# Moving the value splits and the clearing of the block-diagonal values of a rotary attention into the last turn of the cross-attention before it

## What is computed

```python
x = x + _L1_xattn_ref(_layernorm(x, axis=-1), ctx_1024, L1_xattn_Wq, ...)
x = x + _L1_attn_ref(_layernorm(x, axis=-1), L1_attn_Wq, ..., L1_attn_Wo, L1_attn_bo)
# _L1_attn_ref, 16 heads of 64:
q = _apply_rope((x @ Wq + bq).reshape(b, s, H, L), cos, sin)
k = _apply_rope((x @ Wk + bk).reshape(b, s, H, L), cos, sin)
v = (x @ Wv + bv).reshape(b, s, H, L)
attn = softmax(where(causal, q @ k.T / sqrt(L), -1e9))
return (attn @ v).reshape(b, s, H * L) @ Wo + bo
```

## Time and profile before

| | us |
|---|---|
| median of three executions | 1123.29 |
| lowest, highest | 1121.62, 1125.1 |
| the profiled execution, its own time | 1119.95 |
| its span, first to last instruction | 1118.2 |
| matmul busy in the span | 1062.4 (95%) |
| VectorE, ScalarE, GpSimd busy | 639.4, 346.6, 214.2 |

### The profile page before, as it was taken

One profiled execution on the slowest core, in us unless ns is written; L12 is line 12 of the kernel. 1 busy time (PEld: TensorE's weight loads), 2 busy tenths in 40 slices (PEclk: granted clock), 3 DMA queues, 4 the chain that ended last, 5 costly groups with the idle time before them and its releaser, 6 DMA issues.

```text
span 1118.2 us, 16788 instructions
## 1 busy us (share of the span) xinstructions
PE 1062.4 (95%) x6152; PEld 662.9 (59%) x6152; DVE 639.4 (57%) x1105; ACT 346.6 (31%) x982; POOL 214.2 (19%) x205
## 2 busy tenths in 40 slices
PE   7999999999899999999999999999789999999777
PEld 4466658888444444444444565559479796878233
DVE  2454346787756621456751354476756758477667
ACT  1232246666420000220000132244412525135443
POOL 0111101333122221000004311124204132130004
PEclk9999999999999999999999999999899999999899
DMA  9966902001025690025537579941000000040001
GB/s 335 386 250 220 367 3 76 1 1 39 19 93 184 128 38 1 0 91 181 151 103 273 185 264 372 349 169 51 1 1 1 1 0 0 1 166 1 1 1 75
DMA packets 67585, 128.01 MB, mean 114 GB/s; under 512 B 9296, under 2 KB 13136, under 8 KB 67152
## 3 DMA queue, kind: packets, MB, share of 16 engines
q1 hardware_dynamic: 67536, 127.38, 35.4%
HBM read 120.92 MB, written 6.44 MB: 114 GB/s over the span
## 4 chain that ended last, share of the span: by engine, by line
PE 69%; issue 11%; DVE 8%; POOL 5%; SPq 2%; DMA 2%; ACT 1%; POOLq 0%; DVEq 0%; ACTq 0%
PE bank L2075 24%; PE bank L449 5%; PE bank L2102 5%; PE bank L937 4%; PE bank L419 4%; PE bank L380 3%; PE bank L2284 3%; PE bank L944 2%; PE bank L1623 2%; PE bank L1554 2%; PE bank L494 2%; PE bank L483 2%; DMA xres<-in_x_dram 1%; PE bank L953 1%; PE bank L1563 1%
## 5 line engine op out<-in xcount | busy, mean ns | idle before, releaser
L2120 ACT ACTIVATE f_act<-bank,f_sgn 128x512 f32<-128x512 f32 x64 | 44.0, 687 | 266.1 <-PE bank L2075 253.8
L2075 PE MATMUL bank<-f_a_lo,f_w 128*128 128x512 f16 x512 | 115.7, 379 | 0.0
L2075 PE MATMUL bank<-f_a_hi,f_w 128*128 128x512 f16 x512 | 115.7, 379 | 0.0
L2075 PEld LDWEIGHTS bank<-f_a_lo,f_w 128*128 x512 | 50.1, 98 | 60.4
L2075 PEld LDWEIGHTS bank<-f_a_hi,f_w 128*128 x512 | 50.1, 98 | 60.2
L2174 DVE CAST f_b_hi<-f_act 128x512 f16<-128x512 f32 x32 | 26.1, 817 | 96.3 <-ACT f_act L2120 96.3
L1833 DVE TENSOR_TENSOR s_e<-s_pair,s_tables 128x512 f32<-128x512 f32 x64 | 41.4, 689 | 44.2 <-POOL s_qT L1912 15.2
L419 PE MATMUL bank<-x_cT,x_qT 128*64 128x512 f32 x256 | 60.1, 613 | 0.0
L449 PE MATMUL bank<-x_cN,x_eT 128*64 128x512 f32 x256 | 56.9, 596 | 0.0
L1712 ACT ACTIVATE s_e<-bank,s_nmax 128x64 f32<-128x64 f32 x128 | 38.1, 337 | 33.4 <-DVE s_nmax L1775 33.2
L2223 POOL TENSOR_SCALAR f_w<-f_upper_bits 128x2048 bf16<-128x2048 uint8 x16 | 30.8, 1928 | 81.8 <-PE bank L2075 81.8
(11 more groups left out here) (331 smaller groups left out, 2304.9 us busy)
## 6 DMA issues: line engine op xcount, KB each, us to landing
x_cT<-in_ctx_cols_dram SPq DMA_DIRECT2D x32, 1024.0 KB, 9.0
x_cN<-in_ctx_rows_dram SPq DMA_DIRECT2D x32, 1024.0 KB, 10.9
f_upper_bits<-in_f_w_dram SPq DMA_DIRECT2D x20, 256.0 KB, 3.9
f_row<-in_f_wg_dram SPq DMA_DIRECT2D x11, 256.0 KB, 3.5
f_long_row<-in_f_wd_dram SPq DMA_DIRECT2D x4, 704.0 KB, 5.9
f_row<-in_f_wu_dram SPq DMA_DIRECT2D x11, 256.0 KB, 2.8
f_part<-in_f_wgT_dram SPq DMA_DIRECT2D x8, 352.0 KB, 3.5
f_part<-in_f_wuT_dram SPq DMA_DIRECT2D x8, 352.0 KB, 3.4
```

The costliest lines, as they stand in the source:

```text
L2075: mm = pe.matmul(h_bank[s][:, :], weights(2 * i + s, k), part[:, k, cols], start=(n == 0 and k == 0), stop=(n == 1 and k == k_chunks - 1))
L2120: act.activation(act32[s][:, :], h_bank[s][:, :], ACT.Relu, scale=sgn[:, layer % 2:layer % 2 + 1]).then_inc(h_read, 1)
```

## The change

- The clearing of `v_diag` moves from the start of the rotary attention (GpSimd) into the cross-attention's last turn, behind the two bias additions L779 and ahead of the two additions L1351. Its semaphore moves with it.
- High part 2 goes ahead of the copy L551 of the second tile's transposed weights, parts 3 and 4 ahead of the two scaled outputs; only part 5 is left behind the casts L572.
- Low parts 1 to 4 are made ahead of L710, and part 5 ahead of both last additions to x.
- Low part 6 moves from VectorE ahead of step 3 to GpSimd behind its eight rotary steps, ahead of `rstd`.
- The high value weights and the raw and low output weights swap places, so the output weights now lie on the second tile's context rows and their load waits for `av_done, TILES`.

```diff
@@ sync, cross-attention
                 successor.load_values(sp)
-                sp.wait_ge(av_done, TILES - 1)
+                sp.wait_ge(av_done, TILES)
                 successor.load_outputs(sp)
@@ scalar, cross-attention, loop over s with the exponentials
+                    if s == 1 and last and successor is not None:
+                        act.wait_ge(s_done, TILES)
+                        successor.split_hi(act, 2)
                     if proj is None:
                         act.wait_ge(eT_done, 2 * i + s + 1)
                         act.copy(eT[s][:, :, :], as_chunks(bank[ET_BANK[s]][:, :])).then_inc(eT_ok, 1)
@@
                 for s in range(2):
                     if last and successor is not None:
-                        act.wait_ge(s_done, TILES)
-                        successor.split_hi(act, 2 + s)
+                        successor.split_hi(act, 3 + s)
                     act.wait_ge(av_done, 2 * i + s + 1)
@@
                 if last and successor is not None:
-                    successor.split_hi(act, 4)
                     successor.split_hi(act, 5)
@@ vector, cross-attention
                 if last and successor is not None:
-                    for n in range(1, 4):
+                    for n in range(1, 5):
                         successor.split_lo(dve, n)
@@
                 for s in range(2):
-                    if s and last and successor is not None:
-                        successor.split_lo(dve, 4)
+                    if s == 0 and last and successor is not None:
+                        successor.split_lo(dve, 5)
                     dve.wait_ge(y_done, 2 * i + s + 1)
@@ gpsimd, cross-attention
                 pool.wait_ge(successor.small_in, 16 * successor.N_SMALL)
+                pool.wait_ge(xn_ok, TILES + 1)
+                pool.wait_ge(xb_ok, TILES)
+                successor.clear_values(pool)
                 for s in range(2):
                     pool.wait_ge(xn_ok, TILES + s + 1)
                     successor.add_bias(pool, xres, s)
@@ RotaryFront
+    def clear_values(self, pool):
+        pool.memset(self.v_diag[:, :, :, :, :], 0.0).then_inc(self.set_ok, 1)
@@ vector, rotary attention
-            dve.wait_ge(set_ok, 1)
+            dve.wait_ge(rot.set_ok, 1)
@@
                 for n in range(2 * GROUPS):
-                    if first and n in (1, 3):
-
-                        rot.split_lo(dve, 5 + n // 2)
                     if n in (4, 5):
@@ gpsimd, rotary attention
-            pool.wait_ge(*x_done)
-            pool.memset(v_diag[:, :, :, :, :], 0.0).then_inc(set_ok, 1)
-
@@
+                if first:
+                    rot.split_lo(pool, 3 * NB)
                 if last:
                     ffn.roots(pool, 0, 0, TILES - 2)
```

More of the change, by code:

```diff
@@ L1251, in __init__ @@
             self.wv_raw = first("wv_raw", [P, KC, F])
+            first("over_v_hi", [P, KC, F])
             self.wo_raw = first("wo_raw", [P, FC, D])
-            for n in ("over_v_hi", "over_k_hi"):
-                first(n, [P, KC, F])
+            first("over_k_hi", [P, KC, F])
             Front.reserve(first, "raw_over_front")
@@ L1260, in __init__ @@
             self.wk_lo, self.wq_lo, self.wq_hi, self.wv_lo = (sb(n, [P, KC, F], F32R) for n in ("wk_lo", "wq_lo", "wq_hi", "wv_lo"))
+            self.wv_hi = sb("wv_hi", [P, KC, F], F32R)
             self.wo_lo = sb("wo_lo", [P, FC, D], F32R)
-            self.wv_hi, self.wk_hi = (sb(n, [P, KC, F], F32R) for n in ("wv_hi", "wk_hi"))
+            self.wk_hi = sb("wk_hi", [P, KC, F], F32R)
             Front.reserve(sb, "over_front")
@@ L1292, in __init__ @@
         self.xb_ok = sem("xb_ok")
+        self.set_ok = sem("values_cleared")
         self.k_done = sem("k_done")
@@ L1489, in rotary_attention @@
         xT_done, xhi_ok, xlo_ok = front.xT_done, front.xhi_ok, front.xlo_ok
-        set_ok = sem("set_ok")
         q_done = sem("q_done")
```

## The result

The changed kernel takes 1115.34 us (median of five executions, 1112.75 to 1116.6) against 1121.62 us for the kernel before (five executions, 1120.14 to 1125.1). The ratio is 0.9946, with a 95% interval of 0.9923 to 0.9969, so 6.1 us faster. A second set gave 0.993 (0.9905 to 0.9955). The forecast was 1120.9 us, 2.4 faster, in a range of 1116.9 to 1124.6: the direction was right, the size was not. It counted from 1123.29 us, the median of three executions of the kernel before; two more put that median at 1121.62. The profiled execution took 1112.75 us, with a span of 1111.0 against 1118.2.

What follows compares the result with a forecast made beforehand. TensorE, 69% of the span's chain, was taken to wait for VectorE and GpSimd at the rotary attention's start. Rotary side -3.3 plus cross-attention +0.9 gave -2.4: 1120.9 us against the median 1123.29, range 1116.9 to 1124.6.

Steps and rivals of the forecast that it cites:

- The clearing leaves the start: Start of the rotary attention: VectorE's first products start at 762.6 instead of 764.53 us, -1.9.
- Two low parts leave the loop: Rotary loop on VectorE: steps 0 to 1 and 2 to 3 each take 2.9 us, -2.0 twice.
- Low part 6 on GpSimd: Behind the last rotary step: the split takes 4.5 us, holds VectorE's key spreading, and gives back 4.1 of 7.7.
- rotary side: Rotary attention until VectorE goes on behind the third score group: -7.7 without any hindrance, -3.3 with the split.
- third rival: Low part 6 on GpSimd takes longer than 4.5 us; at 8.3 the sum is +1.4, 1124.7 us; chance 0.13.
- the second: Rival: GpSimd's split holds nothing up or is short; sum between -6.8 and -5.4 us; chance 0.12.
- The clearing arrives in the cross-attention: Cross-attention: the clearing holds VectorE's scaling, an L1351 goes before low part 0, clipping L671 ends later; +0.9 us.
- The first rival: Cross-attention: the clearing lets the scaling pass, -0.7 instead of +0.9; sum -4.0, 1119.3 us; chance 0.20.
- a little: Cross-attention: what the faster return of TensorE's clock may give back of the +0.95 us, leaving +0.9.

Runs made afterwards that it cites:

- e4: The changed kernel with GpSimd starting low part 6 only after all eight key spreadings of the turn; 0.99 of the kernel before.
- e2: The changed kernel with the clearing behind the two L1351 additions instead of ahead of them; 0.9974 of the kernel before.
- e10: The changed kernel with the clearing between the two bias additions L1351; executed once, only its profile used: scaling 1.79 us, clipping ends 6.52 behind the scores.
- e5: The kernel before with nine throwaway transposes in TensorE's wait for the low part of x, cross-attention's last turn; 0.9989 of the kernel before.
- e9: The kernel of e2 with nine throwaway transposes in TensorE's wait ahead of the key group; 0.9979 of the kernel before.

## Why the prediction was wrong

- **The clearing leaves the start:** -1.9 predicted, -1.93 measured. **Two low parts leave the loop:** -4.0, and -3.90. Right.
- **Low part 6 on GpSimd:** 4.5 us predicted, 4.55 measured; the spreading held from the split's start to its end, as said. Against the kernel before, the columns spr1 and spr3 grow by 2.76, predicted 2.6 (-5.9 to -3.3). Where the split holds nothing (e4), the rotary side is -7.76, predicted -7.7. The whole rotary side of the change is -3.07 against -3.3. Right, and with it the third rival (a long split) and the second (a split that holds nothing) are out. The Trainium skill, SBUF — State Buffer, section "Who interferes with whom", says that the ports which VectorE and GpSimd share are locked by one of them at a time, and that the order of issue decides who waits. The 4.909 us agree; for the order, the scaling of e2 does not (last section). The 4497 ns that the prediction cites from the Trainium skill are given there for an addition; the subtraction here took 1% longer.
- **The clearing arrives in the cross-attention: this step failed.** It said that "GpSimd's first L1351, queued before low part 0, goes next: 1.26, to 736.1", and took +0.9. Measured is -0.83. I had taken the order from the scaling's end: VectorE's low part was to follow only when the held scaling was through, and by then GpSimd's addition would be queued. The runs show (e2, e10) that a scaling held by a clearing holds nothing behind it. The rule which the prediction cites from that section of the Trainium skill, that a GpSimd operation that only writes leaves two-input operations alone, is borne out by the 2.28 us of low part 0 beside the clearing. Its other half, that VectorE's two-port modes do contend with such an operation, fits the 0.65, 1.79 and 3.03; that this scaling ran in such a mode no run shows. I read both halves right and still put the low part in the wrong place of the queue. The first rival had the sum nearly right (-0.7) by luck: it let the scaling pass, and the scaling was held.
- **The clock in the key group was left out,** but for "a little". It is -1.49 in the profile: with the sooner clipping TensorE loses one of its two waits and stays at 2.4 GHz (e5 and e9 show the same from a filled wait, in one profile each). So the sooner clipping was worth 2.3 us, 0.83 by itself and 1.49 by the clock.
- **The output projection** (-1.53 in the pair of profiles) is no effect of the change: the same kernel shows both times.
- Sum by the steps: -3.07 - 0.83 - 1.49 = -5.4 us, against 6.1 measured (3.5 to 8.6, the interval times 1121.62) and -2.4 predicted. The 3.0 us between sum and forecast are the failed step (1.7) and the clock (1.5), less the 0.2 too much on the rotary side.
- The forecast in absolute time was off by more (1120.9 against 1115.34) because it counted from a median of the kernel before that five executions put 1.7 us lower.

## What to carry to other kernels

Where work goes to GpSimd because it is idle there, look at what VectorE reads at that time, not at GpSimd's own gaps: the same 4.55 us cost a stall of 4.2 beside two-input work and nothing some 9 us later. Where operations of VectorE and GpSimd hold one another, write down the issue times, not the ends, and ask of each GpSimd operation whether it reads SBUF or only writes: the clearing held the scaling, and not the low part behind it. And price a wait of TensorE twice, once by its length and once by the matmuls behind it at the lower clock.

## What the hardware showed that I had not expected

- A VectorE scaling of 8 elements held by a GpSimd clearing lasted 0.65, 1.79 or 3.03 us, until the clearing's end each time, while the next VectorE operation, with two SBUF inputs, started 0.07 us behind it (or when the last reading GpSimd operation had ended) and took its usual 2.28. The records of two VectorE operations overlap by all of the wait.
- In e2 the scaling was issued at 739.00, behind an addition of GpSimd that ended at 740.25, and the clearing only at 740.19; still the clearing took its usual 1.81 and the scaling ended with it, at 742.03 (3.02 us in e9, the same order). So the order of issue alone did not say which of these two goes first. Why is open.
- Waits of 0.71 and 1.14 us, with 0.66 us of transposes between them, were followed by 1.2 GHz in the next key group, in both profiles that have them; one of 0.79 to 1.09 alone was not, in nine, nor were 0.71 and 0.16 with the transposes between, in two. The 1.94 us ahead of the output projection were followed by it in four profiles of eleven.
- The steps of kernels that are alike there agree within 0.04 us, up to the last rotary products and where the clock agrees; the spread of some 7 us between executions of one kernel goes roughly with the granted clock (before: 1117.86 us at a mean of 0.988, 1124.49 at 0.98; but both 1117.8 and 1122.28 at 0.985).
